# Moving a sign flip to GpSimd and two layer-norm steps to ScalarE in a three-layer macaron kernel

## What is computed

```python
def _layernorm(x, axis=-1, eps=1e-5):
    m = jnp.mean(x, axis=axis, keepdims=True)
    v = jnp.var(x, axis=axis, keepdims=True)
    return (x - m) / jnp.sqrt(v + eps)

def ffn(x):                                   # w is complex, 1024 x 1024
    return real(ifft(einsum('bnd,do->bno', fft(x), w))) + bias

def attn(x):                                  # q = x @ wq, k = v = x, by heads
    pre = tril(einsum('bhnd,bhdm->bhnm', q, k))
    return einsum('bhnm,bhmd->bhnd', pre, v)

x = x + 0.5 * ffn(layernorm(x))
x = x + attn(layernorm(x))
x = x + 0.5 * ffn(layernorm(x))
```

## Time and profile before

| what | us |
|---|---|
| median of 3 runs | 3398.32 |
| the three runs | 3276.69, 3475.82, 3398.32 |
| the profiled execution, device time | 3276.69 |
| its slowest core's span (core 7) | 3275.2 |
| spans of the eight cores | 3251.8 to 3275.2 |
| mean granted TensorE clock of core 7, share of full speed | 0.806 |

### The profile page before, as it was taken

One profiled execution on the slowest core, in us unless ns is written; L12 is line 12 of the kernel. 1 busy time (PEld: TensorE's weight loads), 2 busy tenths in 40 slices (PEclk: granted clock), 3 DMA queues, 4 the chain that ended last, 5 costly groups with the idle time before them and its releaser, 6 DMA issues.

```text
span 3275.2 us, 28803 instructions; the slowest of 8 cores (3251.8 to 3275.2 us)
## 1 busy us (share of the span) xinstructions
PE 2095.4 (64%) x11360; PEld 1046.4 (32%) x11360; DVE 1108.9 (34%) x804; ACT 320.2 (10%) x441; POOL 34.4 (1%) x68
## 2 busy tenths in 40 slices
PE   0788889925755685468546854685468646765665
PEld 0333334412342243125312531252126212621252
DVE  1100000034254415441544154415442444244433
ACT  1000000011110101110111011101110110101010
POOL 0000000000000000000000000000000000000000
PEclk9999999967777787778767876787678767877787
DMA  6000000020001000100010001000100010001000
GB/s 205 0 0 1 1 1 1 1 79 0 1 1 52 1 1 1 51 1 1 1 52 0 1 1 51 1 1 1 52 0 1 1 52 1 1 11 41 0 1 26
DMA packets 23855, 56.50 MB, mean 17 GB/s; under 512 B 4016, under 2 KB 4272, under 8 KB 23728
## 3 DMA queue, kind: packets, MB, share of 16 engines
q1 hardware_dynamic: 18608, 37.89, 3.9%
q0 software_dynamic: 5120, 16.78, 1.5%
HBM read 37.88 MB, written 16.78 MB: 17 GB/s over the span
## 4 chain that ended last, share of the span: by engine, by line
PE 60%; DVE 18%; issue 11%; ACT 5%; DMA 4%; SPq 2%; DVEq 0%; ACTq 0%; POOL 0%; POOLq 0%
PE ps_att L480 13%; PE ps_rot L480 9%; PE ps_att L211 8%; DVE sqt L405 5%; PE ps_rot L211 5%; PE ps_scr L545 4%; PE ps_att L475 4%; DVE bufB L434 3%; PE ps_att L466 3%; PE ps_rot L475 3%; DMA bufA<-xT 3%; DVE sqt L399 3%; PE ps_scr L211 3%; ACT bufH L437 2%; PE ps_att L596 2%
## 5 line engine op out<-in xcount | busy, mean ns | idle before, releaser
L402 PE MATMUL ps_rot<-sqt,s_ones 128*128 128x512 f32 x48 | 49.1, 1126 | 379.2 <-DVE sqt L399 379.2
L545 PE MATMUL ps_scr<-bufE,bufB 64*128 64x128 f32 x1024 | 158.4, 315 | 19.4 <-ACT bufF L529 12.5
L405 DVE TENSOR_REDUCE sqt<-bufG 128x512 f32<-128x4096 f32 x24 | 169.1, 7047 | 0.0
L466 PE MATMUL ps_rot<-bufH,sMh 128*128 128x512 bf16 x192 | 62.7, 459 | 152.2 <-ACT bufH L437 152.2
L490 DVE SCALAR_TENSOR_TENSOR ftmp<-ps_att,isrep 128x512 f32<-128x512 f32 x80 | 55.3, 691 | 307.4 <-PE ps_att L480 303.7
L545 PEld LDWEIGHTS ps_scr<-bufE,bufB 64*128 64x128 f32 x1024 | 144.9, 222 | 33.3 <-issue 33.3
L399 DVE TENSOR_REDUCE sqt<-bufA 128x512 f32<-128x4096 f32 x16 | 114.4, 7147 | 121.0 <-DMA bufA<-xT 119.6
L480 PE MATMUL ps_att<-bufH,sMl 128*128 128x512 bf16 x640 | 151.2, 379 | 0.0
L480 PE MATMUL ps_att<-bufI,sMh 128*128 128x512 bf16 x640 | 151.2, 379 | 0.0
L441 DVE SCALAR_TENSOR_TENSOR bufI<-bufB,bufH 128x2048 bf16<-128x2048 f32 x48 | 110.0, 2292 | 110.9 <-ACT bufH L437 92.7
L572 DVE SCALAR_TENSOR_TENSOR scsb<-ps_scr,iscol,smask 128x1024 f32<-128x1024 f32 x64 | 80.0, 1280 | 190.9 <-PE ps_scr L545 190.8
(11 more groups left out here) (156 smaller groups left out, 2897.4 us busy)
## 6 DMA issues: line engine op xcount, KB each, us to landing
bufA<-xT SPq DMA_DIRECT2D x64, 256.0 KB, 8.5
outT<-bufC POOLq DMA_DIRECT2D x64, 256.0 KB, 8.6
sWtmp<-wrt SPq DMA_DIRECT2D x8, 512.0 KB, 15.9
sWtmp<-wit SPq DMA_DIRECT2D x8, 512.0 KB, 10.2
sCh<-cosh SPq DMA_DIRECT2D x8, 256.0 KB, 5.9
sCl<-cosl SPq DMA_DIRECT2D x8, 256.0 KB, 7.9
sNh<-sinh SPq DMA_DIRECT2D x8, 256.0 KB, 9.4
sNl<-sinl SPq DMA_DIRECT2D x8, 256.0 KB, 10.3
```

The costliest lines, as they stand in the source:

```text
L405: cstep(VE, lambda e: e.tensor_reduce(sqt1[:, :].unsqueeze(2), g4, axis=mybir.AxisListType.X, op=ALU.add), reads=["bufG:a", "bufG:b"], wri ...
L466: last = e.matmul(slot, wh[:, 1024 * kb + 128 * db:1024 * kb + 128 * (db + 1)], fb(bufH, kb), start=(kb == 0), stop=False)
L545: return e.matmul(ps_scr[0:128, 128 * h:128 * h + 128], kv, q, start=(h % 4 == 0), stop=(h % 4 == 3), tile_position=(64 * half, 0))
```

## The change

Four edits, all in which engine does a step:

1. A constant `s_epsc`, 128x1 float32 holding 1e-5, is set by VectorE at the very start, in the step that sets the ones.
2. The sign flip of block j (line 234, eight times) is issued on GpSimd rather than VectorE. Operands and waits are the same.
3. `murep` (line 412, 24 times) is computed by ScalarE, as an Identity activation with scale 1/1024 that reads `ps_rot`.
4. Adding 1e-5 (line 421, 24 times) is done by ScalarE, as an Identity activation in place on `isrep` whose bias is read from `s_epsc`.

```diff
+        s_epsc = E0(nc.sbuf_tensor("s_epsc", [128, 1], F32))
...
-        cstep(VE, lambda e: e.memset(s_ones[:, :], 1.0), writes=["s_ones"])
+        cstep(VE, lambda e: (e.memset(s_ones[:, :], 1.0),
+                             e.memset(s_epsc[:, :], EPS))[-1], writes=["s_ones"])
...
-                cstep(VE, lambda e, j=j: (e.tensor_scalar_mul(
+                cstep(GP, lambda e, j=j: (e.tensor_scalar_mul(
                     ih3[:, :, 128 * j:128 * (j + 1)],
                     ih3[:, :, 128 * j:128 * (j + 1)], -1.0),
                     e.tensor_scalar_mul(
...
-            cstep(VE, lambda e: e.tensor_scalar_mul(murep[:, :], ps_rot[:, 0:512], 1.0 / D),
-                  reads=["psR"], writes=["murep"])
+            cstep(SC, lambda e: e.activation(murep[:, :], ps_rot[:, 0:512],
+                                             AF.Identity, scale=1.0 / D),
+                  reads=["psR", "acttab"], writes=["murep"])
...
-            cstep(VE, lambda e: e.tensor_scalar_add(isrep[:, :], isrep[:, :], EPS),
-                  reads=["isrep"], writes=["isrep"])
+            cstep(SC, lambda e: e.activation(isrep[:, :], isrep[:, :], AF.Identity,
+                                             bias=s_epsc[:, 0:1]),
+                  reads=["isrep", "acttab"], writes=["isrep"])
```

## The result

| | before | after |
|---|---|---|
| median of 12 runs each, us | 3309.85 | 3371.61 |
| lowest, us | 3264.47 | 3327.28 |
| profiled execution: slowest core's span, us | 3275.2 | 3338.9 |
| start of the first layer norm, mean of 8 cores, us | 717.8 | 773.7 |
| from there to the end, mean of 8 cores, us | 2545.2 | 2554.3 |

The ratio is **1.0187, 95% interval 1.0158 to 1.0217**. On the 3276.7 us of the profiled execution that is 61 us more, or 3338 us, and the profiled execution of the changed kernel has a span of 3338.9 us. The forecast was 3312 us, 1.1% more. The direction was right, and the size was not: 61 us instead of 35.

A forecast was written before the change was run, and what follows sets the result against it. A chain going from engine to engine, TensorE 60% and VectorE 18% of it, was taken to bound the kernel. Flip 21.0, clock 4.6 and 1e-5 9.8 sum to 35.4 us on 3276.7, giving 3312.1 us; range 3283 to 3350.

The forecast's parts named there:

- The flip: Sign flip on GpSimd, eight times, on the path: two instructions of P, hop 0.2 us; 2.63 us a block, 21.0 us.
- P: Time of one GpSimd multiplication of 128x1024 bf16 in the flip, bounded between about 0.39 and 6.7 us, taken as 1.6 us.
- The clock: mmPi after 4.2 us of idle time: TensorE's clock falls in two blocks of eight, 2.3 us each, 4.6 us.
- rival D: Shift changes when the clock falls elsewhere; some of mmPr's falls spared, up to 10 us back, 3302 us; chance 0.10.
- murep: Mean moved to ScalarE in the layer norm, 24 times: hidden, with 3.9 us of cover, and gives nothing back.
- 1e-5: Addition moved to ScalarE in the layer norm, on the path: reciprocal 0.41 us later, 24 times, 9.8 us.
- three signs: P outside 1.0 to 2.6 us, the clock falling in all blocks, or murep on ScalarE ending after the reduction L405.
- A: Flip on GpSimd slow, P from 2.6 us: over 2% slower, 3348 us at P = 3, 3407 at 6.7; chance 0.11.
- the case of P between 2.0 and 2.6: Flip on GpSimd with P in this range and most clock falls: whole kernel around 3335 us; chance 0.07.
- B: Flip on GpSimd nearly as fast as on VectorE, P at most 1.04, and clock holds: 3297 us; chance 0.18.
- C: Layer norm gives 20 us back if L417 is held by VectorE, not TensorE, with cheap flip: 3277 us; chance 0.02.
- the forecast: Main case, P 1.2 to 2.0 us and few to half of the clock falls: whole kernel 3312 us; chance 0.52.

The follow-up runs named there:

- the probe: Kernel before, plus GpSimd multiplications by -1 on scratch at the very start; one takes 2.75 us for 1024 elements, 1.46 for 512, 0.82 for 256.

## Why the prediction was wrong

**What bounds the kernel**: right. GpSimd's 44 us went fully onto the chain, and VectorE's relief was worth nothing.

**The flip**: here it failed. Its place, its lack of cover and what waits for it were right. The size of P, the time of one GpSimd instruction, was not: 1.6 us taken, 2.75 measured, and with it the term was 38.3 us instead of 21.0. The lower candidates were rows of other engines that spend about 1.0 and 1.7 ns on an element; GpSimd spends 2.5. That such an engine "should be no better than the slower of these" was a bound from below, 1.76 us, and a value under it was then taken; the other end, 6.7 us, was right to name and got too little weight. With P = 2.76 the prediction's own formula gives 8 x (5.52 - 0.77 + 0.2) = 39.6 us, where the wait grew by 38.3; so the hop was sized too large rather than too small. The Trainium skill (GPSIMD Engine Reference, Performance versus the Vector engine) has 1.8 cycles an element as its best case, the 1.54 us of the prediction's estimate, and its section When to use GPSIMD lets one-input operations run at roughly the line rate; the probe has 2.5 ns an element, by an estimate three cycles of the 1.2 GHz that the page gives, and the measurement decides. Its advice to keep elementwise work on VectorE is borne out, by a factor of 7.

**The clock**: 4.6 us taken, about 19 measured. Two things went wrong. With the real P the idle time is 6.3 us and not 4.2, and at 6.3 the first matmuls are slow in every block. And even for 4.2 us "two in eight" was probably too low: after 3.3 us already 11 of 16 blocks started slow, while 4.2 itself was not measured. The trace before could have warned of this. The prediction read the clock at 147 to 148 us and took from it that the fall came within 4.1 us; the stretch before that is

```profile
146.00:147.00 1.00, 0.00 (x0) 0.00 (x0) 1.00 (x3) 0.00 (x0) 0.00 (x0) 0.68 0.00 0
```

so the fall came between 3.1 and 4.1 us into that wait. In the changed kernel it came between 4.3 and 5.3 us into the wait (the 0.85 above). By the first wait 4.2 us is past the fall, by the second short of it, so one row of one wait was too little to decide. Of rival D, by which `mmPr` would give something back, little came: its first 48 matmuls took about 0.5 us a block less on five cores and 0.3 to 0.5 more on three, 1.4 us less in all on the mean. The sum closes: 38.3 us for the wait, 17.2 more in `mmPi`, 1.4 less in `mmPr`, together 54.1, and 55.9 were measured.

**murep**: right in place and size. It ends 3.8 us before it is needed; the run with this edit alone has 1.0002.

**1e-5**: 9.8 us predicted. The chain shows 0.97 - 0.64 = 0.33 us rather than 0.41 (hops of 0.15 and 0.10 us and an activation of 0.72), 7.9 us for 24; the stage shows 8.0 and the runs 0.28%, 9 us. The clock took nothing more, as predicted: the first 20 matmuls of the second part of `dense` took 157.0 us in sum and 156.4 before. The Trainium skill (ScalarE: Activation LUTs, What ACT_TABLE_LOAD costs) gives 93 ns for an operand read through a pointer, and the trace agrees: 0.72 us for the 1e-5 with it, 0.63 for the square root of the same shape without.

**The rivals**: the prediction named three signs by which it would be wrong. Two came: P outside 1.0 to 2.6 us, and a clock that falls in all blocks. They are the conditions of A, which had 0.11. A's formula gives 8 x (2 x 2.75 - 0.77 + 0.2) + 18 + 9.8 = 67 us, 3344; 61 were measured, 1.9% and not clearly over A's 2%. That 3338 us lies near the case of P between 2.0 and 2.6 ("around 3335 us"), and inside the range of 3283 to 3350, is no merit of either: P was above that case, and the range reached so far only to hold A's near side. The median of all twelve runs, 3371.61, lies above the range. B, C and the forecast fell. The two mistakes, 17 us in the wait and 14 in the clock, were not independent, since a slower flip lengthens the very wait in which the clock falls. The chances had treated them as if they were. (In the stages both kernels differ by 65 us; 35.4 forecast, 17 and 14 more for these two, and 2 less for the 1e-5 make the same 65.)

## What to carry over

An operation that the trace has never shown on an engine has no row to lean on: before it goes on the path, measure it there, or move it off the path, where its price no longer matters (here 44 us of GpSimd work cost nothing once they ran ahead of the loop). A wait in front of TensorE that grew from 1.5 to 6.3 us cost twice here, once as waiting and once as matmuls at the low clock, and of 12.7 us saved ahead of a TensorE that restarts at the low clock 7.0 were lost to it again. Look for work that fits into a wait that stays in any case, not for an engine that is idle.

## What the runs showed of the hardware

- GpSimd multiplies 128 partitions by a constant at 2.5 ns an element a partition plus about 0.18 us, alike for bf16 and float32 input and for pieces of 128 elements, with bf16 output (the probe).
- TensorE's first eight matmuls took 1.9 to 2.1 us after 1.4 to 1.5 us of idle time (all eight cores), 2.5 to 3.6 us in 11 of 16 blocks after 3.3 us, and 3.2 us or more in all blocks after 5 us and more. At 6.3 us it was GpSimd that TensorE waited for, in the other cases VectorE.
- Taking 0.53 us off the way to each `dense` saved 12.7 us. While TensorE restarted at the low clock, 7.0 us of them came back in the 20 matmuls after its wait; with fillers in the wait these matmuls took 7.8 us less.
